# The order of work under a 64-step recurrence: setup groups, expert units and routing placed in other gaps, a norm on GpSimd

## Time and profile before

| | |
|---|---|
| three runs | 1205.8, 1205.84, 1207.82 us (median 1205.84) |
| profiled execution | 1204.1 us, of it 1202.3 us span |
| busy, share of span | PE 84%, PEld 57%, DVE 62%, ACT 36%, POOL 43% |
| first logits | 42.7 us |
| last tanh of the recurrence | 607.46 us |
| last unit added | 738.8 us |
| mean granted TensorE clock | 0.867 of full |

### The profile page before, as it was taken

How to read it: one execution, slowest core, us unless ns; L and a number is a source line. 1 busy time by engine, 2 the same in 40 slices (tenths; PEclk the granted TensorE clock), 3 DMA queues, 4 the chain that set the end, 5 groups by cost and what they waited for, 6 DMA issues and landing times. The chain is left out here.

```text
span 1202.3 us, 29942 instructions
## 1 busy us (share of the span) xinstructions
PE 1011.9 (84%) x12380; PEld 680.1 (57%) x12380; DVE 748.8 (62%) x1882; ACT 432.3 (36%) x794; POOL 512.3 (43%) x452
## 2 busy tenths in 40 slices
PE   3588667699988899989986996899999999997967
PEld 2477555555554455544542442677776777775545
DVE  5645544645476555775578565678777777875453
ACT  1211012122121222222221221677777777775111
POOL 4688300022232333223333554566666666664010
PEclk9555555579998999989999998999999999999878
DMA  9020026022221222213221441000000000000000
GB/s 245 11 66 1 1 45 123 1 76 67 58 54 36 76 70 54 69 26 88 71 71 53 126 122 36 2 3 3 2 3 3 2 3 2 3 3 2 1 18 17
DMA packets 46059, 51.58 MB, mean 43 GB/s; under 512 B 22086, under 2 KB 36584, under 8 KB 45928
## 3 DMA queue, kind: packets, MB, share of 16 engines
q1 hardware_dynamic: 43010, 48.71, 15.7%
q10 hardware_dynamic: 2918, 1.01, 0.5%
HBM read 48.13 MB, written 1.57 MB: 41 GB/s over the span
## 5 line engine op out<-in xcount | busy, mean ns | idle before, releaser
L639 POOL TENSOR_TENSOR ex<-ex,xn 128x512 f32<-128x512 f32 x128 | 162.5, 1270 | 354.0 <-DVE ex L1168 255.1
L798 ACT ACTIVATE thcb<-ps 128x512 f32<-128x512 f32 x132 | 78.8, 597 | 286.0 <-PE ps L1514 285.1
L704 POOL TENSOR_TENSOR wu<-encC,wu 128x1024 f16<-128x1024 f32 x64 | 137.7, 2167 | 56.4 <-ACT encC L871 56.4
L1163 DVE SCALAR_TENSOR_TENSOR ex<-thcb,ps 128x512 f32<-128x512 f32 x132 | 90.5, 686 | 98.9 <-ACT thcb L798 96.9
L1521 PE MATMUL ps<-ex,wd 128*128 128x512 f32 x256 | 142.3, 639 | 1.9 <-POOL ex L639 1.9
L1514 PE MATMUL ps<-xnT,wg 128*128 128x512 f16 x384 | 111.0, 400 | 8.4 <-DVE ex L1168 8.4
L1514 PE MATMUL ps<-xnT,wu 128*128 128x512 f16 x384 | 111.2, 401 | 0.0
L1463 PEld LDWEIGHTS ps<-eb,encC 128*128 128x128 f16 x3072 | 87.7, 99 | 32.6 <-issue 16.3
L1574 PE MATMUL ps<-wg,M 128*128 128x128 f16 x1536 | 98.2, 222 | 2.1 <-DVE wg L1257 2.1
L1574 PEld LDWEIGHTS ps<-wg,M 128*128 128x128 f16 x1536 | 93.0, 99 | 6.9 <-DVE wg L1257 2.5
L1168 DVE TENSOR_TENSOR ex<-ex,ps 128x512 f32<-128x512 f32 x132 | 90.7, 687 | 7.2 <-POOL ex L639 2.8
(11 more groups left out here) (292 smaller groups left out, 1846.2 us busy)
## 6 DMA issues: line engine op xcount, KB each, us to landing
xn<-coef_rows SPq DMA_DIRECT2D x128, 256.0 KB, 3.8
thcb<-in_L_ffn_Wg SPq DMA_DIRECT2D x8, 256.0 KB, 3.2
thcb<-in_L_ffn_Wu SPq DMA_DIRECT2D x8, 256.0 KB, 3.1
wd<-in_L_ffn_Wd SPq DMA_DIRECT2D x2, 1024.0 KB, 10.0
xtok<-in_x SPq DMA_DIRECT2D x4, 256.0 KB, 6.4
thcb<-in_ctx SPq DMA_DIRECT2D x2, 512.0 KB, 11.2
wu<-in_L_xcond_attn_wq SPq DMA_DIRECT2D x2, 512.0 KB, 10.8
wu<-in_L_xcond_attn_wk SPq DMA_DIRECT2D x2, 512.0 KB, 10.6
```

What stands on the lines that cost most here:

```text
L639: nc.gpsimd.tensor_tensor(hid[:, n % 2, :], gu[:, n % 2, :], other, ALU.mult)\
L704: nc.gpsimd.tensor_tensor(z[:, 1, 8 * u:8 * u + 8, :], a_Zc[:, u], z[:, 0, 8 * u:8 * u + 8, :], ALU.subtract)\
L798: nc.scalar.activation(th[:, n % 2, :], bank(n % 2), ACT.Tanh, scale=0.5 / WSCALE)\
L1163: V.scalar_tensor_tensor(ga[:, :], th[:, n % 2, :], 1.0, bank(n % 2), add, mul)\
```

## The change

- **Setup groups** go at one per place 0 and one per place 3 (`slots`). Of the products for M, the first five alternate with the norm group and the four Wv transposes; the last two alternate with the products for N. A product is evacuated as float16 by ScalarE in place 0, and VectorE only subtracts, in place 1. So are the four context groups before the recurrence. Splits move to place 2, the last eight from gaps 56 to 63 to one a step in steps 15 to 22; the stop scans move to gaps 27, 39, 51 and 58, the norm scales into the second chunk.
- **Units** go behind the logits (place 0) and behind the state product (place 3), numbered through over the chunks, with their pass two gaps later (places 2 and 1) and their down product four or five gaps later (places 3 and 1), ahead of a new unit in that place. The first stands at gap 96 instead of 92, the last at 359 instead of 346.
- **diag** is made from an identity in PSUM instead of SBUF.
- **Prologue**: other gaps; the norm is two GpSimd instructions over 128x512; the halves of the normed tile are made by ScalarE (two copies) and GpSimd (a subtraction); x1 is transposed before the statistics.
- **Routing**: the 32 MAX8 become nine `tensor_tensor` passes of maximum or minimum over halves, and the comparisons go over all four token tiles at once. 43 counted VectorE instructions instead of 74.

```diff
+        products, transposes = groups[N_RNN + 8:], []
+        for n, product in enumerate(products):
+            groups.append(product)
+            if n < len(transposes):
+                groups.append(transposes[n])
+                n_wvT = len(groups) - 1
+        while late_M or folded:
+            groups.extend(folded[:1] + late_M[:1])
...
-        setup_sem = ["setup_dve" if splits(g) or g >= N_RNN and g % 2 else "setup_act" for g in range(N_SETUP)]
+        setup_sem = ["setup_dve" if splits(g) else "setup_act" for g in range(N_SETUP)]
...
-        late_gaps = [*range(0, 33, 2), *(gap for gap in range(34, 50) if gap % IDLE_GAPS)]
+        slots = [0, 3, 4, 7, 8, 11, 12, 15, *(x for st in range(4, 12) for x in (4 * st, 4 * st + 3)), 48, 51, 52, 55, 56]
+        def out_gap(slot):
+            return slot + (slot % IDLE_GAPS == 3)
-        SPLITS = {**{4 * c + 3: c for c in range(SHARED + 1)}, **{56 + i: SHARED + 1 + i for i in range(8)}}
+        SPLITS = {4 * (c if c <= SHARED else c + 6) + 2: c for c in range(WEIGHTS)}
...
-        STOPS = {40: 0, 44: 1, 48: 2, 52: 3, 56: "sum", 57: "count", 58: "keep", 60: "scales"}
-        PRO = {0: "project", 1: "residual", 2: "stats", 5: "norm", 6: "x1T", 7: "xn2T", 9: "router",
-               **{gap: ("route", i) for i, gap in enumerate(g for g in range(10, 26) if g % IDLE_GAPS)}, 26: "coefT"}
+        STOPS = {27: 0, 39: 1, 51: 2, 58: 3, 59: "sum", 61: "count", 62: "keep", GAPS + 9: "scales"}
+        PRO = {0: "project", 2: "residual", 4: "x1T", 6: "stats", 10: "xn2T", 12: "router", 13: "sig0", 14: "sig1", 15: "sig2",
+               16: "sfc", 18: "top1", 19: "top2", 20: "more", 22: "rank", 23: "mask", 26: "pick", 27: "csum", 28: "inverse",
+               30: "coef", 31: "coefT"}
-        U0 = 28
-        unit_gap = [U0 + 2 * min(n, PAIRS - 1) for n in range(UNITS)]
+        U0 = 32
+        def unit_gap(m, n):
+            q = m * UNITS + n
+            return GAPS + U0 + IDLE_GAPS * (q // 2) + 3 * (q % 2)
+        def down_gap(m, n):
+            return unit_gap(m, n) + (4 if (m * UNITS + n) % 2 else 5)
+        PASS_AT = {gap + 2: u for gap, u in UNIT_AT.items()}
...
+            def part(m, p):
+                if p == "stats":
+                    t.settle(nc.gpsimd.tensor_tensor(rstd[:, :], mv[:, :, 1], k_eps.broadcast_to([P, TPC]), ALU.add))
+                    t.settle(nc.gpsimd.tensor_tensor(xn2c[:, :, :], x1c, mv[:, :, 0].unsqueeze(2).broadcast_to([P, TPC, P]),
+                                                     ALU.subtract))
+                    t.settle(nc.gpsimd.tensor_tensor(rstd[:, :], rstd[:, :], k_rsqrt.broadcast_to([P, TPC]), ALU.pow))
+                    nc.gpsimd.tensor_tensor(xn2c[:, :, :], xn2c[:, :, :], rstd[:, :].unsqueeze(2).broadcast_to([P, TPC, P]),
+                                            ALU.mult).then_inc(s["norm_ready"], 1)
...
-                    V.tensor_scalar(diag[r, :], ident[r, r], rsum[r, :], 2.0, mul, mul)\
+                    V.tensor_scalar(diag[r, :], bank(Y_BANK)[r, EYE], rsum[r, :], 2.0, mul, mul)\
...
-                    for g in range(G):
-                        pt.mark(V.max(gtop[:, t, g, :], sfc[:, t, g * GE:(g + 1) * GE]))
+                elif p == "top1":
+                    a, b = grouped(sfc)[:, :, :, 0:4], grouped(sfc)[:, :, :, 4:8]
+                    pt.mark(V.tensor_tensor(hi, a, b, ALU.max))
+                    pt.settle(V.tensor_tensor(lo, a, b, ALU.min))
...
+            for at, k, st, place, p in schedule():
+                if k < CH:
+                    rnn(k, st, place)
+                if at in LATE:
+                    setup(LATE[at])
...
+                part(k - 1, p)
+                if at in DOWN_AT:
+                    down(*DOWN_AT[at])
+                if at in UNIT_AT:
+                    unit(*UNIT_AT[at])
```

More of the change, by code:

```diff
@@ L440, in build @@
         UNITS = PAIRS + 1
-        U0 = 28
-        unit_gap = [U0 + 2 * min(n, PAIRS - 1) for n in range(UNITS)]
-        END_GAP = unit_gap[-1] + 6
-        def units_at(gap, m, tail, delay=0):
-            return [(chunk, n) for chunk, g in ((tail, gap + GAPS), (m, gap)) if chunk is not None
-                    for n in range(UNITS) if unit_gap[n] + delay == g]
-        def others(m, n):
-            if isinstance(m, int) and m == 0 and n < 2:
-                return None
-            return m * UNITS + n - (1 if n else 0)
@@ L473, in build, with side, schedule @@
+        def side(m, n):
+            return (m * UNITS + n) % 2
+        def schedule():
+            for at in range(END):
+                k, gap = divmod(at, GAPS)
+                yield at, k, gap // IDLE_GAPS, gap % IDLE_GAPS, PRO.get(gap) if 1 <= k <= CH else None
         block = ctx.enter_context(nc.Block())
@@ L823, in _ @@
             all_evacuated(act, N_RNN - 1)
-            stages(act, stage)
+            for at, k, st, place, p in schedule():
+                if k < CH and place == 0:
+                    rnn_exp(k, st)
+                elif k < CH and place == 3:
+                    rnn_tanh(k, st)
+                if at in SPLITS:
+                    c = SPLITS[at]
+                    landed(act, c)
+                    nc.scalar.activation(halves_of[c][0], landing_view(c), ACT.Copy, scale=WSCALE)\
+                      .then_inc(s["weights_hi"], 1)
+                for g in late_out(at, 0):
+                    setup(g)
+                part(k - 1, p)
+                if at in UNIT_AT:
+                    unit(*UNIT_AT[at])
             act.wait_ge(s["x2_ready"], CH)
@@ L1433, in _ @@
             pe.wait_ge(s["consts_ready"], 2)
+            mm(bank(Y_BANK)[:, EYE], same[:, :], ident[:, 0:B], start=True, stop=True).then_inc(s["eye_ready"], 1)
             def x_parts(t):
@@ L1520, in down @@
                 pe.wait_ge(s["hid_ready"], m * UNITS + n + 1)
[L1521 removed]
+                mm(bank(5), wd[:, n, :] if n < PAIRS else swd[:, :], hid[:, side(m, n), :],
                    start=(n == 0), stop=(n == UNITS - 1)).then_inc(s["y_ready"], 1)
[L1524 to L1542 removed]
+            for at, k, st, place, p in schedule():
+                if k < CH:
+                    rnn(k, st, place)
+                if at in LATE:
+                    setup(LATE[at])
+                if STOPS.get(at) == "count":
+                    pe.wait_ge(s["flags_ready"], 1)
+                    mm(bank(3)[:, 0:NT], upto[:, :], flags[:, :], start=True, stop=False)
+                    mm(bank(3)[:, 0:NT], same[:, :], excl[:, :], start=False, stop=True).then_inc(s["cnt_ready"], 1)
+                part(k - 1, p)
+                if at in DOWN_AT:
+                    down(*DOWN_AT[at])
+                if at in UNIT_AT:
+                    unit(*UNIT_AT[at])
             pe.wait_ge(s["att_w_in"], 16 * ATT_DMAS)
```

312 lines of the change are left out of this document (138 added, 174 removed).

## The result

The changed kernel takes 1243.28 us in the median (1237.7 to 1250.28, 4 runs) against 1205.82 of the kernel before on the same chip: ratio 1.031, 95% interval 1.0251 to 1.037. It is slower; the forecast was 1174, the range 1150 to 1190. The profiled execution is 1240.18 us with a span of 1238.5.

The account below looks back on a forecast made before the run. No engine is full; the order of the queues and the recurrence's chain were taken to bound it. -3.0 -25.5 -7.8 +2.1 -5 -1.5 +9.2 = -31.5: 1172.6 against 1204.1, 1174 against the median; range 1150 to 1190.

Parts of the forecast that it names:

- Parts 1 to 3: Before the first step, rest of the first chunk, prologue without units: -3.0, -25.5 and -7.8 us.
- rivals 2 and 4: 2: clock rises early, 1140 us, 9%. 4: first chunk gains half, 1187 us, 17%.
- Part 4: Steps with units: TensorE waits 0.8 us before a down product, step 7.87 against 7.69; stretches +2.1, -5, -1.5 us.
- Part 3: Prologue without units, 64.5 us: eight steps of 5.67 and fillings make 56.7, so -7.8 us.
- The port: Between VectorE and GpSimd: one product (1.27 us) charged to top and to rank; by the skill's rule another 4 us.
- Part 5: After the recurrence: 52 units left at 2.15 us each, 140.5 us in all, +9.2.
- rival 3: Unit steps: standstill of 0.8 us lowers the clock, 5.3 us a step; all 39 +200, a fifth gives 1214; 4%.
- rival 1: Unit steps: the down product doesn't wait, step 7.0 us, 0.87 less in 39 steps, -34, 1140 us; 8%.

Follow-up runs that it names:

- e8: Changed kernel with the unit ahead of the down product in place 3 only in the tail, behind the last tanh: 1212.0 us.
- e5: e2 with the residual's normalisation moved back from GpSimd to VectorE, four passes at gap 8: 1177.0 us.
- e11: e5 with the residual's statistics moved from gap 6 to 3 and the normalisation from gap 8 to 7, both in place 3: 1169.3 us.
- e2: Changed kernel with TensorE issuing the unit ahead of the waiting down product in place 3, tail too: 1184.2 us.
- e1: Changed kernel with the down product of each odd unit one gap later, in place 0 and not 3: 1204.3 us.
- e4: Changed kernel with the units back at their old places 0 and 2, down product five gaps behind: 1180.9 us.
- e3: Changed kernel with three thrown-away products of 512 columns ahead of the waiting down product in place 3, recurrence only: 1231.4 us.
- e9: e2 with an additional thrown-away VectorE pass of 512 columns ahead of diag from step 24 on: 1214.1 us.
- e12: e4 with the same additional VectorE pass ahead of diag as in e9, from step 24 on: 1237.7 us.
- e10: Changed kernel with one thrown-away product, not three as in e3, ahead of the waiting down product in place 3: 1236.0 us.

## Why the prediction was wrong

**Right.** Parts 1 to 3: first tanh 46.19 (near 47), tanh 15 at 163.11 (near 162), the clock at 0.50 up to the first unit, so rivals 2 and 4 did not come; the gain there is 33.4 us of the 36.3 forecast. In Part 4 the new wait is where it was put and released by GpSimd; it is 0.50 us by the profile instead of 0.8, and the step without a fall is 7.98 us against 7.87. Two sums of the prediction are off without weight: the terms of Part 3 add to 57.0 and not 56.7, and a prologue among units before the change was 22 us by its own figures (146.08 less 124), not 19. The port: the pass charged with one product of GpSimd is this one, by its line (count, duration least, median and most, in ns):

```profile
L1138 DVE TENSOR_TENSOR gtop<-sfc x4: 285/1372/1372, 200.3 to 638.2; 128x128 f32<-128x128 f32 x4
```

The run at 200.3 us has no GpSimd beside it and takes 0.285 us, later ones 1.37: +1.09, and one pass of the rank shows the same (L1155, 256 elements: 0.42 us once and 1.37 three times, mean 1.13, where the earlier trace rows has 0.425). 1.27 had been charged to each. The Trainium skill (SBUF — State Buffer, "SBUF: two separate sides") has the lock hold a VectorE instruction with two SBUF inputs for the whole GpSimd instruction; the trace agrees for the one pass that meets it, and the further 4 us that I had worked out for all routing passes did not come.

**Wrong, first: Part 5.** The step that failed is "The price of a unit is GpSimd's 1.27 + 0.89 = 2.15, the same as TensorE's 1.29 and 0.86". That is what an engine needs for a unit, and it holds if TensorE always has other work while a unit's chain runs. The earlier trace rows were taken under an order with one unit and one down product more between a unit and its own down product. The places 3 and 0 leave the recurrence with the gaps numbered on, and in the tail, where nothing else stands in the gaps, the pair of units has one unit and one down product of cover for tanh, pass and product. 2.95 and not 2.15 a unit: +33.5 us against the forecast, of which e8 gives back 27.0 by order alone (174.0 to 146.9). Taking the norm off GpSimd brings the tail to 136.3 and 135.3 (e5, e11), below the forecast 140.5.

**Wrong, second: rival 3 was the case, and I gave it 4%.** The step that failed is "against: the waits of today are as long". They are (0.69 us ahead of diag in the earlier trace rows), with 4 falls of 21; but the new wait came with 15. The sum had no fall in these steps: 21 of 7.87 us are 165.3 us, and they took 192.4, or 27.1 more. Of this, 24.0 are 15 falls of 1.6 us (9.62 less 8.02), the rest is a step of 8.02. The other 19 steps add 4.2, which makes the 31.3 us by which the stretches with units lie above the forecast. Rival 3 had the mechanism but not its size: it charged 5.3 us to a step with a fall, three times what one cost, and asked for a clock below 0.8 where 0.86 to 0.88 came. e2 shows the size the other way: without the wait, the recurrence from tanh 23 is 22.7 us shorter, from fewer falls and a step of 7.3 and not 8.0. That is rival 1's step too: "unit steps near 7.0" was 7.22 in e2, so the places themselves are good, and one down product in the wrong order spent what they gained. The 0.2% that the prediction took as the noise was too small as well: 13 executions of the kernel before, taken beside e1 to e4, lie between 1202.85 and 1213.13 us.

**Third: the norm on GpSimd,** charged with 1.6 us net in a prologue. In e2, without the other waits, it is a standstill of 2.82 us with low clock behind it, and it takes e5 and e11 together to be rid of it: 14.9 us by the medians, and here the intervals of e2 and e11 just meet at 0.974.

**Settled and open.** Shown: falls are added by a standstill of TensorE within steps that are otherwise full. Taking it away (e1, e2), or covering it with useless products at the same step length (e3), takes most of the added falls away; adding one to e2 or e4 (e9, e12), at another instruction, brings as many. Not shown: why the kernel before bears 0.69 us ahead of diag with 4 falls while e10, with 0.29 us ahead of a down product, has 13. With the units apart, 0.36 and 0.50 us a step (e4, before) gave 5 and 4 falls and 0.94 gave 14; side by side, 0.14 gave 5 and 0.35 gave 13. That suggests that the placement shifts how much is borne, but no run changed it alone with the standstill kept, and each count is from one execution. Nor is it known why 5 to 7 falls (e2, e5, e11) stay where the steps without a fall have TensorE busy 7.12 of 7.22 us.

## What to carry to other kernels

When work is moved to other gaps, count for each chain (unit, tanh, pass, GpSimd's product, down product) how much of TensorE's own list stands between its first and last product, once with the recurrence in the gaps and once without: here one swap of two calls in one queue was worth 59 us. A wait on TensorE has two prices, its own length and the clock behind it. Here 0.5 us of wait made a step 0.7 us longer (8.02 against 7.33 us in e2), and a fall cost 1.6 us where it came; ten more falls in 21 steps are another 0.8 us a step. The second price was as large as the first, so a wait that the sum shows as harmless deserves more than a few per cent. And an instruction whose input comes from another engine belongs behind the chain's own instructions of that gap, not ahead of them (e5 to e11: 7.7 us between the medians, with intervals that overlap; 11.5 us of recurrence by the traces).

## What was not expected of the hardware

- The clock fell in steps where TensorE had stood still for no more than 0.3 to 0.6 us at a time (15, 13 and 13 of 21 steps in the changed kernel, e9 and e10). The Trainium skill (TensorE: Matmul & The Clock Gate, Part 1) has activity release a throttle that is the default. The first 221 us here speak against that alone: TensorE is busy 105.4 of 116.9 us in the first chunk and its clock stays at 0.50 (1.2 GHz), while the units lift it at once: the first one's two halves take 1.46 and 0.91 us (225.46 and 226.72 us), and the first three steps with units have a granted clock of 0.69, 0.80 and 1.00.
- At one and the same step length, more work made a higher clock: 15 falls with 0.62 us of standstill a step, 8 with 0.15 (e3).
- GpSimd needs 1.01 us for a power of 4 elements per partition (L669), as long as for a subtraction of 512 (1.04 us, L667).
